# An attention and mixture-of-experts block: GpSimd's DMAs tied to the running tile, the last batch's norms on VectorE, the last exponential on ScalarE

## What is computed

```python
x = x + attention(layernorm(x), ln1_g, ln1_b, Wq, Wkv, Wo, ln2_g, ln2_b)   # ends in its own layer norm
t = layernorm(x)
probs = softmax(t @ gate_w.T)                    # 8 experts
topw, sel = top_k(probs, 2); topw /= sum(topw)
gate, up = split(einsum('th,efh->etf', t, gate_up_w))
expert_out = einsum('etf,ehf->eth', up * gelu(gate), down_w)
out = x + sum over the two chosen experts of topw * expert_out
```

## Time and profile before

| what | value |
| --- | --- |
| median of 3 runs | 641.99 us (641.37 to 643.72) |
| the profiled execution's own time | 646.65 us |
| its span, first to last instruction | 644.9 us |
| TensorE busy | 579.1 us, 90% |
| VectorE busy | 413.0 us, 64% |
| GpSimd busy | 398.0 us, 62% |
| ScalarE busy | 304.7 us, 47% |

### The profile page before, as it was taken

How to read it: one execution, slowest core, us unless ns; L and a number is a source line. 1 busy time by engine, 2 the same in 40 slices (tenths; PEclk the granted TensorE clock), 3 DMA queues, 4 the chain that set the end, 5 groups by cost and what they waited for, 6 DMA issues and landing times. The chain is left out here.

```text
span 644.9 us, 8672 instructions
## 1 busy us (share of the span) xinstructions
PE 579.1 (90%) x2569; PEld 331.9 (51%) x2569; DVE 413.0 (64%) x783; ACT 304.7 (47%) x576; POOL 398.0 (62%) x327
## 2 busy tenths in 40 slices
PE   2799999999999998989999988999956879799990
PEld 1455455444554453445455444444423768688880
DVE  2767658658747978775696888565866465244433
ACT  2235554445546554354646434465362634355540
POOL 4337686668668855697785669778665455533331
PEclk9779999999999999889999999999987989899995
DMA  5121011010110100050000000000044101231005
GB/s 170 53 81 67 2 67 68 0 68 0 68 49 19 67 2 2 4 217 9 2 1 1 1 6 20 10 1 2 7 139 121 36 16 39 63 80 28 24 15 195
DMA packets 23981, 29.29 MB, mean 45 GB/s; under 512 B 4403, under 2 KB 14901, under 8 KB 23936
## 3 DMA queue, kind: packets, MB, share of 16 engines
q1 hardware_dynamic: 21664, 24.50, 11.5%
q0 software_dynamic: 2272, 4.24, 2.0%
HBM read 13.73 MB, written 15.32 MB: 45 GB/s over the span
## 5 line engine op out<-in xcount | busy, mean ns | idle before, releaser
L980 ACT ACTIVATE prob<-s_ps 128x512 f32<-128x512 f32 x256 | 150.6, 598 | 186.6 <-PE s_ps L1073 182.7
L906 DVE TENSOR_REDUCE rowmax<-max_ps 128x1 f32<-128x512 f32 x256 | 173.5, 686 | 90.5 <-PE max_ps L1042 88.4
L843 POOL TENSOR_TENSOR fold<-prob 128x1024 f32<-128x1024 f32 x63 | 149.8, 2378 | 93.6 <-ACT prob L980 93.1
L1087 PE MATMUL pv_ps<-prob,v 128*64 128x512 f32 x512 | 139.7, 626 | 0.0
L1071 PE MATMUL s_ps<-q_hl,khh 128*128 128x512 f32 x256 | 119.5, 467 | 1.1 <-ACT prob L980 0.7
L1042 PE MATMUL max_ps<-khh,q_hl 128*128 128x512 f32 x256 | 106.2, 423 | 8.4 <-DVE q_hl L895 4.4
L1073 PE MATMUL s_ps<-q_hm,kly 65*128 65x512 f32 x256 | 102.9, 402 | 0.0
L1071 PEld LDWEIGHTS s_ps<-q_hl,khh 128*128 128x128 f32 x256 | 49.3, 193 | 80.7 <-ACT prob L980 59.1
L849 POOL TENSOR_TENSOR psums<-fold 128x512 f32<-128x512 f32 x63 | 82.0, 1301 | 4.9
L1042 PEld LDWEIGHTS max_ps<-khh,q_hl 128*128 128x128 f32 x256 | 50.8, 199 | 29.2 <-DVE rowmax L906 9.8
L1073 PEld LDWEIGHTS s_ps<-q_hm,kly 65*128 65x128 f32 x256 | 49.6, 194 | 9.1 <-issue 3.4
(11 more groups left out here) (202 smaller groups left out, 779.9 us busy)
## 6 DMA issues: line engine op xcount, KB each, us to landing
sorted_rows<-blank SPq DMA_DIRECT2D x36, 260.0 KB, 2.6
raw_early<-in_gate_upT SPq DMA_DIRECT2D x6, 512.0 KB, 5.9
wd<-in_downT SPq DMA_DIRECT2D x8, 256.0 KB
raw_early<-parts SPq DMA_DIRECT2D x8, 256.0 KB, 4.1
psums<-sorted_rows SPq DMA_DIRECT2D x22, 65.0 KB, 1.8
xs_first<-sorted_rows SPq DMA_DIRECT2D x17, 65.0 KB, 1.8
x<-in_x SPq DMA_DIRECT2D x4, 256.0 KB, 5.3
raw_w<-in_gate_upT SPq DMA_DIRECT2D x2, 512.0 KB, 3.1
```

Source lines behind the costliest of these rows:

```text
L843: nc.gpsimd.tensor_tensor(fold[:, :, :], prob[:, head % 4, 0:2, :], prob[:, head % 4, 2:4, :], ALU.add).then_inc(prob_folded, 1)
L906: nc.vector.tensor_reduce(rowmax[:, group % 2, it, i:i + 1], max_ps[:, k % 2, :], AX_X, ALU.max).then_inc(max_done, 1)
L980: nc.scalar.activation(prob[:, head % 4, jt, :], s_ps[:, k % 2, :], ACT.Exp, scale=SCALE).then_inc(exp_done, 1)
L1087: last = nc.tensor.matmul(pv_ps[DH * hd:DH * hd + DH, :], v[:, b % 2, jt, :], prob[:, head % 4, jt, :], start=(jt == 0), stop=(jt == JT - 1))
```

## The change

Five things. `POOL_LOW` gets expert 3, so GpSimd makes four experts' low weights and VectorE four. On VectorE the statistics of y move behind all low weights and the first `x_low`. The last batch's two norms go to VectorE (`last_norms`): it reads y in its PSUM bank, takes off the mean and multiplies by g2, and adds to x after multiplying by rstd; only the power that makes rstd stays on GpSimd. ScalarE has no YT, YADD and XNORM of the last batch any more. The last batch's exponential is ScalarE's, as in the other batches, where GpSimd raised e to a power; ScalarE had its Gelu table loaded by then. GpSimd waits in every turn from 3 on for the weighing of tile k-3 before it sends anything; before, it did in turns 7 to 14.

```diff
         def after_scalar(act, kind, b, bank):
+            if b == LB and kind in ("YT", "YADD", "XNORM"):
+                return
...
-            if kind == "CHOOSE0" and b < LB:
+            if kind == "CHOOSE0":
                 act.wait_ge(logit_less, b + 1)
                 nc.scalar.activation(pr[:, :, :], pr[:, :, :], ACT.Exp).then_inc(prob_exp, 1)
...
             if kind in ("YSTAT", "XSTAT"):
-                ln_rsqrt(pool)
-            if kind == "YADD":
+                if b == LB:
+                    count["ln_pool"] += 1
+                    pool.wait_ge(ln_stats, count["ln_pool"])
+                    nc.gpsimd.tensor_tensor(rstd[:, :], var_eps[:, :], minus_half[:, :], ALU.pow).then_inc(ln_rstd, 1)
+                else:
+                    ln_rsqrt(pool)
+            if kind == "YADD" and b < LB:
...
-            if kind == "CHOOSE0" and b == LB:
-
-                pool.wait_ge(logit_less, b + 1)
-                nc.gpsimd.tensor_tensor(pr[:, :, :], euler[:, :, :], pr[:, :, :], ALU.pow).then_inc(prob_exp, 1)
...
+        def last_norms(dve, kind, tiles, bank):
+            def moments_of(tile):
+                for t in range(TPB):
+                    last = nc.vector.bn_stats(stats[:, t, :], tile[:, t, :])
+                link(dve, last)
+                for t in range(TPB):
+                    last = nc.vector.bn_aggr(moments[:, t, :], stats[:, t, :])
+                link(dve, last)
+                nc.vector.tensor_scalar(var_eps[:, :], moments[:, :, 1], EPS, None, ALU.add).then_inc(ln_stats, 1)
+                count["ln_dve"] += 1
+                link(dve, nc.vector.tensor_scalar(neg_mean[:, :], moments[:, :, 0], -1.0, None, ALU.mult))
+
+            if kind == "YSTAT":
+                dve.wait_ge(x3_ready, LB)
+                dve.wait_ge(y_added, LB)
+                dve.wait_ge(y_turned, NB)
+                y = bank[:, :].rearrange("p (t d) -> p t d", d=P)
+                moments_of(y)
+                for t in range(TPB):
+                    last = nc.vector.scalar_tensor_tensor(out=z[:, t, :], in0=y[:, t, :], scalar=neg_mean[:, t:t + 1],
+                                                          in1=g2[:, :], op0=ALU.add, op1=ALU.mult)
+                last.then_inc(z_ready, 1)
+            if kind == "YADD":
+                dve.wait_ge(z_ready, NB)
+                dve.wait_ge(ln_rstd, count["ln_dve"])
+                dve.wait_ge(x1_offset, NB)
+                for t in range(TPB):
+                    last = nc.vector.scalar_tensor_tensor(out=tiles[:, t, :], in0=z[:, t, :], scalar=rstd[:, t:t + 1],
+                                                          in1=tiles[:, t, :], op0=ALU.mult, op1=ALU.add)
+                link(dve, last)
+            if kind == "XSTAT":
+                moments_of(tiles)
+            if kind == "XNORM":
+                dve.wait_ge(x3_turned, LB)
+                dve.wait_ge(x3_copied, LB)
+                dve.wait_ge(rows_sent, 16 * TOP_K * TPB * LB)
+                dve.wait_ge(ln_rstd, count["ln_dve"])
+                for t in range(TPB):
+                    last = nc.vector.tensor_scalar(xr[:, 0, t, 0:P], tiles[:, t, :], neg_mean[:, t:t + 1],
+                                                   rstd[:, t:t + 1], ALU.add, ALU.mult)
+                last.then_inc(x3_ready, 1)
...
-            POOL_LOW = (0, 1, 2)
+            POOL_LOW = (0, 1, 2, 3)
...
+                    if k >= 3:
+
+                        pool.wait_ge(eow_ready, k - 2)
                     if k in ROW_SENDS:
-
-                        pool.wait_ge(eow_ready, k - 2)
                         send_rows(k - SEND_AT)
...
                 for e in VECTOR_LOW[:3]:
                     low_gate_up(dve, e, wl_ready)
-                for kind in BEFORE:
-                    after_vector(dve, kind, LB, bank)
                 for e in VECTOR_LOW[3:]:
                     low_gate_up(dve, e, wl_ready)
                 x_low(0)
+                for kind in BEFORE:
+                    after_vector(dve, kind, LB, bank)
```

More of the change, by code:

```diff
@@ L1 @@
-import math
 from contextlib import ExitStack
@@ L217, in bass_preln_mqa_moe_kernel @@
         ones = sb(whole, "ones", [P, P])
-        euler = sb(whole, "euler", [P, TPB, E])
         bases = sb(whole, "bases", [P, E])
@@ L459, in after_vector @@
         def after_vector(dve, kind, b, bank):
             tiles = x1[:, b * TPB:(b + 1) * TPB, :]
-            if kind == "YSTAT":
+            if b == LB:
+                last_norms(dve, kind, tiles, bank)
+            elif kind == "YSTAT":
                 dve.wait_ge(z_ready, b + 1)
                 ln_moments(dve, z)
-            if kind == "XSTAT":
+            elif kind == "XSTAT":
                 dve.wait_ge(y_added, b + 1)
@@ L806, in set_constants @@
                     nc.gpsimd.memset(begun[:, :], 0.0)
-                    nc.gpsimd.memset(euler[:, :, :], math.e)
                     nc.gpsimd.iota(places[:, :], pattern=[[1, REST]], base=0, channel_multiplier=0,
```

## The result

| | median of the runs | runs | profiled execution | its span |
| --- | --- | --- | --- | --- |
| before | 641.66 us (640.94 to 643.72) | 6 | 646.65 us | 644.9 us |
| with the change | 636.63 us (635.05 to 638.56) | 6 | 636.48 us | 634.8 us |

The ratio is 0.9918, 95% interval 0.9897 to 0.9939: 0.8% faster, 5.0 us by the medians, against a forecast of 4.6. The two profiled executions differ by 10.1 us in span, twice as much. Most of what is above 5 is not the change's, as experiment 1 shows: one turn of 6.70 us, 3.83 longer than with the change, belonged to that one execution of the kernel before.

The account below looks back on a forecast made before the run. TensorE, busy 90% of the span, was taken as the bound. 0.25 - 1.35 - 2.0 - 1.5 = -4.6 took the median from 641.99 to 637.4 us; the range ran from half a microsecond beyond 633.5 up to 641.0.

Parts of the forecast that it names:

- a fifth place that could move: Prediction named only four: tiles' start, x3's turning with the logits, the down matmuls' stop, the 6.70 us turn.
- Low weights: Start of the expert tiles: VectorE and GpSimd alternate on SBUF, so tiles begin at 497.8; +0.25 us.
- Norms: Last batch's norms on VectorE: x3's turning loses its 0.98 us wait, the logits their 0.37; -1.35 us.
- Choice: Stop before the down matmuls: exponential on ScalarE, both table loads covered, wait 1.6 us instead of 3.6; -2.0 us.
- Clock: Matmuls behind the down matmuls' stop: full instead of half clock up to gate(7); -1.5 us, bounds 0 and -1.6.
- GpSimd's ties: GpSimd's sends waiting for the weighing in more turns: nothing on the path, 0; the 3.86 us stall left out.
- The stall in all runs: Rival: the late turn's stall is in timed runs and goes with the send burst, another -3.9, 633.5 us; chance 0.22.
- the sends that bring more of them: Rival: sends meeting SP's row loads cause two more stalls of 3.9 us, about 645.2 us; chance 0.05.
- No turn-taking: Rival at the low weights: VectorE and GpSimd do not alternate, another -3.1, 634.3 us; chance 0.05.
- VectorE and ScalarE too full: Rival: x_low late twice, Gelu load uncovered, clock falling after the stop; only -1.5, 640.5 us; chance 0.23.

Follow-up runs that it names:

- experiment 1: Kernel before, unchanged: 643.31 us; kernel before plus only GpSimd's wait in every turn from 3: 643.44 us; changed kernel without those new waits: 636.96 us.
- experiment 5: Changed kernel again: 637.53 us; with row sends two a turn: 636.63; also three low-weight experts on GpSimd: 634.91; also the choice's steps in later turns: 633.86.
- Experiment 4: Changed kernel with GpSimd making three experts' low weights instead of four: 635.95 us; with two: 637.30 us.
- experiment 3: Changed kernel with the last batch's two norms back on ScalarE and GpSimd: 639.37 us, ratio 0.9947.
- Experiment 6: Changed kernel with three low-weight experts on GpSimd, two row sends a turn, later choice, and ScalarE copying turned x3 before turned hidden values: 635.31 us.
- experiment 2: Changed kernel with the last batch's exponential back on GpSimd as a power of e: 643.26 us, ratio 1.0007.

## Why the prediction was right, and where it was off

The total, 4.6 us forecast and 5.0 measured, comes from the terms that were named, and each was read again in a trace. Two readings it began with were wrong and cost it nothing: the granted clock does not dip only near the end (it stands at 7 and 8 in slices 2, 3, 17 and 18 of the earlier trace rows), and there was a fifth place that could move, gate(15) to gate(16) with 4.76 us; experiment 5 took 1.46 from its 4.30 with the change. The ends of the sum, 636.3 to 638.7, are narrower than its own bounds: the clock at 0 alone gives 638.9.

- **Low weights, +0.25.** Measured +0.14. The total was right and the picture behind it was wrong: "The engines take turns" was read as alternation, piece by piece, with VectorE's first three pieces drawn out. Experiment 4 shows VectorE standing for GpSimd's whole row, and one piece drawn out. The sum is the same either way, since the same pieces run one behind the other, but the picture matters for the next edit. The move of the statistics, which is part of this term, was not run by itself. The Trainium skill, page "SBUF — State Buffer", section "SBUF: two separate sides", says that whichever engine starts first holds the shared ports for the whole instruction. The traces agree that the two don't overlap; they show more than that sentence says, for GpSimd had one piece under way at 487.86 and held on through two further ones, until 491.19.
- **Norms, -1.35.** Measured -1.29 in the pair and -1.15 by experiment 3. The 0.98 at x3's turning went as forecast; counted from gate(3) to the start of the turning the gain is 1.16 (2.64 us before, 1.48 with the change). That the term came so near is partly luck: this half gave more than its bracket, the other half nothing. The operations took 1.13 and 1.11 for four, where 1.0 was taken between 0.9 and 1.4. Gate(1) to gate(2) takes 3.34 us where it took 2.82, and the next turn gives it back (2.86 against 3.46). The step that failed is "ScalarE [...] copies yT in time: the logits' 0.37 goes too". Both the copy and TensorE's turning came 1 us sooner, together, and between them on ScalarE's list stands the copy of the hidden values, which the sentence passed over. Experiment 6 shows it.
- **Choice, -2.0 for the stop.** Measured -2.41 in the pair (3.60 to 1.19) and -2.47 by experiment 2 (3.66 to 1.19). `hidden(4)` was due at 515.5 in the frame of before and ended at 514.59, 0.55 us of it from an attention block that ended sooner. The stop was then 1.2 instead of 1.6. Both table loads lasted 1.28 us, 3.0 us with all that lies between them, and TensorE did not wait for Gelu. The Trainium skill, page "ScalarE: Activation LUTs", section "What ACT_TABLE_LOAD costs", gives 1283 ns for the load and 1380 ns more of drain, 2.66 us for a switch. The trace agrees with the load and shows no drain: the first load begins at 510.27 as the copy ahead of it ends (510.25), the exponential at 511.56 as the load ends, and Gelu likewise at 513.27. With the page's drain twice Gelu would, by an estimate, have come 2.8 us later, and `hidden(4)` would have held TensorE; the measurement decides.
- **Clock, -1.5.** Measured -1.50 in the pair, from the weighing to gate(7), and about -1.9 by experiment 2 (4.33 less 2.47). The two differ because the clock fell at different moments: behind the 3.60 us stop of the earlier trace rows the eight down matmuls still ran at full clock (1.15 us), behind the 3.59 and 3.66 us stops of experiments 1 and 2 they did not (2.08 and 2.07). A stop of 1.19 us left the clock at full, so "I take 1.6 to be without one" held; a stop of 1.6 itself was not met.
- **GpSimd's ties, 0.** Measured 0 in both directions, experiment 1. Leaving the stall out of the sum was right, and adding it would have forecast 633.5. The reason given, that the execution it stood in lay 4.66 above the median, is weak by itself: the profiled executions of experiment 1's kernel before and of experiment 4's with two experts lay 2.2 and 3.2 above theirs without any stall.
- **The rivals.** The stall in all runs, and the sends that bring more of them, fell with experiment 1. No turn-taking fell with the +0.14 and with experiment 4. VectorE and ScalarE too full did not come: the granted clock behind the stop was 1.00, and Gelu held nobody.

The parts add up. In the pair 0.14, -1.29, -2.41 and -1.50 make -5.06 us, against 5.0 timed and 4.6 on the other chip (experiment 5). The prices of the experiments, 0.14, -1.15 and -4.33, make -5.3, a little more, by the clock that fell sooner in experiment 2.

## What to carry to other kernels

A stall that stands in one profiled execution should be looked for in a second profile before anything is built on it, above all when that execution lies above the median by about as much. Elementwise work handed to GpSimd to unload VectorE was no help where both read SBUF at the same time: VectorE's piece lasted longer by each GpSimd piece that it overlapped. A slow operation of a few elements on GpSimd can cost twice, by the stop of the engine behind it and by the half clock that follows a long stop (3.6 us here). Two table loads on ScalarE can cost little when the first runs before its data is there and the second ends before its result is needed.

## What the runs showed of the hardware that was not expected

- VectorE's first piece waited for the whole rest of a row of GpSimd instructions, three of them (4.41 us instead of 1.22), and not for the one under way alone. GpSimd's pieces were not drawn out (1256 to 1307 ns).
- VectorE and ScalarE stood 6.5 and 5.2 us with a release the trace calls remote, in one of fourteen profiled executions, while their lists wait there for TensorE's signals alone. Its cause is open.
- GpSimd's power took 5.43 us for 32 elements a lane and 1.05 for 4, ScalarE's exponential 0.23 for the same 32.
- After stops of TensorE of the same length, 3.60 and 3.59 us in two executions of one kernel, the granted clock fell at different moments: in one behind the next eight matmuls (1.15 us), in the other before them (2.08 us).
- A switch of ScalarE's table took 1.28 us, with no gap of more than 0.02 us before or behind it.
